# Perceiver of two layers: the loops of three attention phases written out, and layer 0's first norm moved from VectorE to ScalarE and GpSimd

## What is computed

```python
def _layernorm(x, axis=-1, eps=1e-05):
    m = jnp.mean(x, axis=axis, keepdims=True)
    v = jnp.var(x, axis=axis, keepdims=True)
    return (x - m) / jnp.sqrt(v + eps)

x = x + _L0_xattn_ref(_layernorm(x), ctx_1024, 32, ...)   # one head, softmax over the 32 largest of 257 scores
x = x + _L0_attn_ref(_layernorm(x), ...)                  # 16 heads of 8, rotary positions
x = x + _L0_ffn_ref(_layernorm(x), ...)                   # 8 experts, one each
x = x + _L1_xattn_ref(_layernorm(x), ctx_1024, ctx_1024, ...)
x = x + _L1_attn_ref(_layernorm(x), ...)                  # 16 heads of 64, behind a further RMS norm
x = x + _L1_ffn_ref(_layernorm(x), ...)                   # 8 experts, two each
```

## Time and profile before

| | before |
|---|---|
| median of 3 runs | 1502.33 us (1502.33 to 1504.12) |
| the profiled execution | 1503.75 us |
| its span, first to last instruction | 1502.0 us |
| busy in the span: TensorE, its weight loads | 1330.2 us (89%), 1020.1 us (68%) |
| VectorE, ScalarE, GpSimd | 1056.0 us (70%), 817.4 us (54%), 684.0 us (46%) |
| granted TensorE clock, mean | 0.957 of full speed |

### The profile page before, as it was taken

How to read it: one execution, slowest core, us unless ns; L and a number is a source line. 1 busy time by engine, 2 the same in 40 slices (tenths; PEclk the granted TensorE clock), 3 DMA queues, 4 the chain that set the end, 5 groups by cost and what they waited for, 6 DMA issues and landing times. The chain is left out here.

```text
span 1502.0 us, 42305 instructions
## 1 busy us (share of the span) xinstructions
PE 1330.2 (89%) x14710; PEld 1020.1 (68%) x14710; DVE 1056.0 (70%) x3440; ACT 817.4 (54%) x2416; POOL 684.0 (46%) x1301
## 2 busy tenths in 40 slices
PE   3888888877899969999999999978999999986981
PEld 2666666664577847777777777757788878875960
DVE  3889999864712258888888888865788888784433
ACT  2556665543223348888888888854444444443640
POOL 1455555531156724444444444541224444545773
PEclk9999999997999979999999999999999999997995
DMA  6655643301011132222222222200000000002425
GB/s 191 198 162 178 205 152 121 108 18 57 15 32 33 34 121 80 69 79 72 77 83 65 84 80 69 80 27 2 2 1 12 14 14 11 21 21 80 114 78 174
DMA packets 78431, 113.92 MB, mean 76 GB/s; under 512 B 12480, under 2 KB 55753, under 8 KB 78160
## 3 DMA queue, kind: packets, MB, share of 16 engines
q1 hardware_dynamic: 70352, 97.93, 20.2%
q0 software_dynamic: 6784, 12.06, 2.6%
q10 hardware_dynamic: 1152, 2.10, 0.4%
HBM read 78.95 MB, written 35.00 MB: 76 GB/s over the span
## 5 line engine op out<-in xcount | busy, mean ns | idle before, releaser
L1825 ACT ACTIVATE c_pr<-c_pS,c_nm 128x257 f32<-128x257 f32 x512 | 236.3, 475 | 74.8 <-DVE c_nm L1955 74.2
L1955 DVE TENSOR_REDUCE c_nm<-c_pS 128x1 f32<-128x257 f32 (+1 forms) x384 | 173.4, 507 | 29.9 <-PE c_pS L1694 29.9
L2303 ACT ACTIVATE s_k<-s_pK 128x512 f32<-128x512 f32 x128 | 76.4, 597 | 154.3 <-PE s_pK L2189 154.3
L2189 PEld LDWEIGHTS s_pK<-s_hT,AH 128*128 128x128 f32 x1024 | 123.9, 195 | 20.6 <-ACT s_k L2303 16.7
L2189 PE MATMUL s_pK<-s_hT,AH 128*128 128x128 f32 x1024 | 137.4, 284 | 0.5 <-ACT s_hT L2298 0.5
L1698 PE MATMUL c_pT<-cst,c_pr 128*128 128x128 f32 x1024 | 132.8, 273 | 0.0
L1698 PEld LDWEIGHTS c_pT<-cst,c_pr 128*128 128x128 f32 x1024 | 116.1, 141 | 0.4 <-issue 0.4
L1964 DVE COPY c_prT<-c_pT 128x512 f32<-128x512 f32 x128 | 88.5, 691 | 22.9 <-PE c_pT L1698 22.7
L1825 ACT ACTIVATION_READ_ACCUMULATOR c_pr<-c_pS,c_nm 128x1 f32 x512 | 104.0, 203 | 0.0
L2216 PE MATMUL s_pM<-BH,s_uT 128*128 128x128 f32 x832 | 98.2, 275 | 0.0
L2216 PEld LDWEIGHTS s_pM<-BH,s_uT 128*128 128x128 f32 x832 | 95.5, 192 | 0.0
(11 more groups left out here) (388 smaller groups left out, 3375.2 us busy)
## 6 DMA issues: line engine op xcount, KB each, us to landing
rows_in<-c_blank SPq DMA_DIRECT2D x32, 520.0 KB, 3.3
a_ctxT<-in_ctxT SPq DMA_DIRECT2D x32, 514.0 KB, 3.6
c_ctxT<-in_ctxT SPq DMA_DIRECT2D x128, 128.5 KB, 2.2
a_ctxN<-in_ctxR SPq DMA_DIRECT2D x32, 512.0 KB, 4.3
hb<-rows_in SPq DMA_DIRECT2D x39, 130.0 KB, 2.3
f_w<-in_f_w SPq DMA_DIRECT2D x16, 256.0 KB, 3.4
a_ctxL<-in_ctxL SPq DMA_DIRECT2D x128, 16.0 KB, 3.7
f_w<-in_f_w SPq DMA_DIRECT2D x16, 128.0 KB, 3.4
```

Source lines behind the costliest of these rows:

```text
L1825: act.activation(pr[:, b % 2, c, :], pS[:, c, 0:S], ACT.Exp, bias=nm[:, c:c + 1], accum_out=den[:, b % 2, c:c + 1]).then_inc(e_ready.sem, 1)
L1955: dve.tensor_reduce(nm[:, c:end], pS[:, c:end, 0:S], AX.X, ALU.max, negate=True).then_inc(max_ready.sem, 1)
L2189: mm = pe.matmul(pK[:, c % 2, i, :], AH[:, c * HK + i, :], hT[:, p, :], start=True, stop=True)
```

## The change

Three things change. In layer 0's attentions all 38 slots are written out, and SyncE's loop too; group numbers and semaphore values become constants. In layer 1's self-attention the five passes are written out. And the first norm of layer 0 is a `ScalarNorm`: ScalarE makes the negated mean and the sum of squared differences with the accumulator of an activation, GpSimd makes 1/sqrt(squares + 128 epsilon) and the shift, mean times that, and ScalarE scales. The missing factor sqrt(128) is put into the copy of the transposed result. VectorE loses three instructions a slot; it only prepares 128 epsilon once. ScalarE now waits at slot 1 for all of x too. On ScalarE the mean of w comes before the copy of the second norm (`normed_a`), the squares behind it, the scaling ahead of the exponentials. On GpSimd the norm step stays first in the slot.

```diff
+class ScalarNorm:
...
+        self.part, self.off = f("part", [P, D]), f("off", [P, D])
...
+    def scalar_mean(self, act, x):
+        act.activation(self.part[:, :], x, ACT.Copy, scale=-1.0 / D, accum_out=self.neg_mean[:, :]).then_inc(self.mean_ready.sem, 1)
+
+    def scalar_squares(self, act, x, r):
+        act.wait_ge(self.mean_ready.sem, self.mean_ready.at(r))
+        act.activation(self.off[:, :], x, ACT.Square, bias=self.neg_mean[:, :], accum_out=self.squares[:, :]).then_inc(self.squares_ready.sem, 1)
+
+    def vector_eps(self, dve):
+        dve.tensor_scalar(self.eps_d[:, :], self.env["k"]("eps"), float(D), None, ALU.mult).then_inc(self.eps_ready.sem, 1)
+
+    def gpsimd(self, pool, r):
+        if isinstance(r, int) and r == 0:
+            pool.wait_ge(self.eps_ready.sem, 1)
+        pool.wait_ge(self.squares_ready.sem, self.squares_ready.at(r))
+        pool.tensor_tensor(self.ve[:, :], self.squares[:, :], self.eps_d[:, :], ALU.add).then_inc(self.ve_ready.sem, 1)
+        pool.wait_ge(self.ve_ready.sem, self.ve_ready.at(r))
+        pool.tensor_tensor(self.rstd[:, :], self.ve[:, :], self.env["k"]("half"), ALU.pow).then_inc(self.rstd_ready.sem, 1)
+        pool.wait_ge(self.rstd_ready.sem, self.rstd_ready.at(r))
+        pool.tensor_tensor(self.shift[:, :], self.neg_mean[:, :], self.rstd[:, :], ALU.mult).then_inc(self.shift_ready.sem, 1)
+
+    def scalar_scale(self, act, x, r):
+        act.wait_ge(self.shift_ready.sem, self.shift_ready.at(r))
+        act.activation(self.h[:, :], x, ACT.Identity, bias=self.shift[:, :], scale=self.rstd[:, :]).then_inc(self.h_ready.sem, 1)
...
-        n1 = Norm(ctx, nc, "a_n1", env)
+        n1 = ScalarNorm(ctx, nc, "a_n1", env)
...
-            peeled = 6
-            for s in range(peeled):
-                slot(*groups(s), s % 2, s // 2)
-            pairs = (G - 1 - peeled) // 2
-            with eng.Fori(0, pairs) as i:
-                for s in (peeled, peeled + 1):
-                    slot(*(i * 2 + g for g in range(s + 1, s - 7, -1)), s % 2, i + s // 2)
-            for s in range(peeled + 2 * pairs, G + 6):
+            for s in range(G + 6):
                 slot(*groups(s), s % 2, s // 2)
...
-            with sp.Fori(1 + E, G // 2 - 1) as i:
+            for i in range(1 + E, G // 2 - 1):
...
-                act.activation(hT[:, :], pX[:, 0, :], ACT.Copy).then_inc(hT_ready.sem, 1)
+                act.activation(hT[:, :], pX[:, 0, :], ACT.Copy, scale=float(D) ** 0.5).then_inc(hT_ready.sem, 1)
...
+            def scale_w(w_):
+                if later(w_):
+                    act.wait_ge(hT_done.sem, hT_done.at(w_ - 1))
+                n1.scalar_scale(act, x_of(w_), w_)
...
             def slot(w_, x, t, u, a, b, z, l, p, r):
+                if isinstance(x, int) and x == 1:
+                    act.wait_ge(env["rest_loaded"], 4 * 16)
...
                 run(turned_weights, u)
+                run(lambda g: n1.scalar_mean(act, x_of(g)), w_)
                 run(lambda a: normed_a(a, p), a)
+                run(lambda g: n1.scalar_squares(act, x_of(g), g), w_)
                 run(sums, u)
...
                 run(queries_by_keys, x)
+                run(scale_w, w_)
                 run(exponentials, t)
...
+            n1.scalar_mean(act, X[:, 0, :])
+            n1.scalar_squares(act, X[:, 0, :], 0)
+            scale_w(0)
             slots(act, slot)
...
-                run(lambda g: n1.vector_rows(dve, x_of(g)), w_)
...
-                run(lambda g: n1.vector_moments(dve, g), w_)
...
-                run(scale_w, w_)
...
-            n1.vector_stats(dve, X[:, 0, :], 0)
-            scale_w(0)
+            n1.vector_eps(dve)
             slots(dve, slot)
...
-            with eng.Fori(1, 6) as i:
+            for i in range(1, 6):
                 for j in range(4):
                     slot(i * 4 + (5 + j), (5 + j) % 2, False, False, True, j, i)
```

More of the change, by code:

```diff
@@ L229, in vector_scale, with __init__ @@
                           ).then_inc(self.h_ready.sem, 1)
+class ScalarNorm:
+    def __init__(self, ctx, nc, name, env):
+        self.env = env
+        f = lambda n, s: ctx.enter_context(nc.sbuf_tensor(f"{name}_{n}", s, F32))
+        self.part, self.off = f("part", [P, D]), f("off", [P, D])
+        self.neg_mean, self.squares, self.ve, self.rstd, self.shift = (f(n, [P, 1]) for n in ("neg_mean", "squares", "ve", "rstd", "shift"))
+        self.eps_d, self.eps_ready = f("eps_d", [P, 1]), Signal(ctx, nc, f"{name}_eps_ready")
+        self.h = f("h", [P, D])
+        self.mean_ready, self.squares_ready = Signal(ctx, nc, f"{name}_mean_ready"), Signal(ctx, nc, f"{name}_squares_ready")
+        self.ve_ready, self.rstd_ready = Signal(ctx, nc, f"{name}_ve_ready"), Signal(ctx, nc, f"{name}_rstd_ready")
+        self.shift_ready, self.h_ready = Signal(ctx, nc, f"{name}_shift_ready"), Signal(ctx, nc, f"{name}_h_ready")
+    def scalar_mean(self, act, x):
[17 more added lines that the diff above has]
+        act.activation(self.h[:, :], x, ACT.Identity, bias=self.shift[:, :], scale=self.rstd[:, :]).then_inc(self.h_ready.sem, 1)
@@ L616, in keep_logits, with x_of @@
                 act.activation(LG[:, bass.ds(z, 1), :].rearrange("p g e -> p (g e)"), pB[:, 2, 0:E], ACT.Copy).then_inc(lg_ready.sem, 1)
+            def x_of(g):
+                return X[:, bass.ds(g, 1), :].rearrange("p g d -> p (g d)")
+            def scale_w(w_):
+                if later(w_):
+                    act.wait_ge(hT_done.sem, hT_done.at(w_ - 1))
+                n1.scalar_scale(act, x_of(w_), w_)
             def slot(w_, x, t, u, a, b, z, l, p, r):
+                if isinstance(x, int) and x == 1:
+                    act.wait_ge(env["rest_loaded"], 4 * 16)
                 run(turned_self_weights, z)
@@ L693, in x_of @@
                 return X[:, bass.ds(g, 1), :].rearrange("p g d -> p (g d)")
-            def scale_w(w_):
-                if later(w_):
-                    dve.wait_ge(hT_done.sem, hT_done.at(w_ - 1))
-                n1.vector_scale(dve, x_of(w_), w_)
             def largest(i):
```

## The result

The changed kernel takes 1491.1 us (median of 4 runs, 1487.79 to 1492.84) against 1503.22 for the kernel before on the same chip: ratio 0.9902, 95% interval 0.9875 to 0.9929. Two later series of six runs gave 0.9885 (0.986 to 0.9909) and 0.9892 (0.9872 to 0.9912). The forecast, 1484.4 of 1502.33, is 0.9881: inside all three intervals, on the faster side of their middle.

The account below looks back on a forecast made before the run. Layer 0's slot was bound by two legs, scale_z to rotation on TensorE and rotation to scale_z on VectorE. Gains 17.4 + 1.1 + 0.1 = 18.6 us gave 1485.1 or 1483.7; forecast 1484.4, between them, range 1480 to 1492.

Parts of the forecast that it names:

- (a): Layer 0's slots 7 to 31 without loop turns, slow slots and loop exit: 11.4 us gained.
- (b): First norm off VectorE in layer 0: its scaling leaves the rotation-to-scale_z leg, 0.25 us a slot, x 24 = 6.0.
- (c): ScalarE's added mean, squares and scaling, 1.48 us a slot, all hide in its idle gaps; nothing starts later.
- (d): GpSimd's longer norm chain still ends before the rotated sum, with 0.14 us to spare: the thinnest cover.
- (e): Start: group 0's norm waits for a table load and two ScalarE passes; counted 0, bounds -0.6 to +1.
- (f): Layer 1's self-attention written out: 0.1 us counted for the loop's entry, bounds -0.5 to +0.7.
- (g): Fetching the straight code: counted 0, upper end 0.56 us a slot.
- Rival 5: The fetch of straight code is not hidden: 13.4 us back, 1497.8; chance 0.03.
- (1): ScalarE's or GpSimd's share does not fit and the norm's gain is given back: 1491.7; chance 0.15.
- (2): The low clock stays, other waits bringing it as often; 3.1 us comes back: 1487.5; chance 0.1.
- (3): Squares need another activation table, two loads a slot on ScalarE: slower, 1518 to 1564; chance 0.03.
- (4): ScalarE's 1.48 us a slot lie on the path in full: 38 us lost, 1529; chance 0.01.

Follow-up runs that it names:

- unroll_only: The kernel before with its loops written out and the first norm left on VectorE; ratio 0.9962 to the kernel before.
- pe_loop_late: The changed kernel with the factor matrices loaded late and the loop back on TensorE alone; ratio 0.994 to the kernel before.
- pe_act_out: factors_late with the loops back on VectorE, GpSimd, SyncE and in layer 1; ratio 0.9918 to the kernel before.
- factors_late: The changed kernel with the loads of the two factor matrices moved to the end of SyncE's layer 0 list; ratio 0.9888 to the kernel before.
- norm_only: The changed kernel with loops back on TensorE, VectorE, GpSimd, SyncE and in layer 1, only ScalarE's list written out; ratio 0.9927 to the kernel before.
- again: The changed kernel run once more, unaltered; ratio 0.9885 to the kernel before.
- act_extra: The changed kernel with three more unused 128x128 copies on ScalarE in every slot; single run 1491.05 us.
- pool_extra: The changed kernel with one more unused 128x1 power on GpSimd in every slot, ahead of the norm's own; single run 1493.12 us.
- again_2: The changed kernel run a third time, unaltered; ratio 0.9892 to the kernel before.

## Why the prediction was right, and where its steps were off

The mechanism was right: two legs to a slot, the third norm's scaling between them, 8.70 without the first norm. Measured: 8.69, with legs of 3.64 and 5.05 where 3.66 and 5.04 were forecast. The whole came out higher than forecast by 2.7 us in the profiled execution (1487.79 for 1485.1), by the 2.9 given back behind layer 1's last slot. That the gain up to rotation 31 met its sum, 18.67 for 18.5, is luck: slots 7 to 31 gave 2.2 less than forecast, and what lies ahead of them 2.4 more.

- **(a)** "Layer 0 without a loop", 11.4: 10.65 in unroll_only. TensorE's loop by itself brings the turn back (pe_loop_late), and the loops of VectorE, GpSimd and SyncE bring none (pe_act_out); ScalarE's was not tried by itself. The 0.09 that a plain slot loses with the loops is on the VectorE leg. Mis-stated was the low clock: the slow slots also go with the norm alone, and one of the two was not there in a second profile of before. As it is in the gains of both parts, they can't simply be added: 10.65 + 8.97 - 3.08 = 16.5; factors_late, without the stall, measures 16.9.
- **(b)** 0.25 a slot: 0.245 in norm_only, 0.25 from unroll_only to the changed kernel. In the medians of one chip the shares came out the other way round, though: the loops alone brought 6.1 us (unroll_only), the norm 10.7 (norm_only), of 17.3 for both (again), where the sums of the prediction have 11.5 and 7.1. Part of it is the low clock: 3.1 us of it went with the norm alone, and unroll_only's profile has 6.5 more behind layer 0.
- **(c)** nothing on ScalarE: right. The scaling took 0.49, near its upper end. The mean with its read took 0.38 and the squares with theirs 0.48, both below their ranges, as a read starts before its activation ends. The gaps held three more copies of 0.30 each (act_extra).
- **(d)** "the thinnest cover": right, with 0.34 to spare, not 0.14, because the squares and their read end 0.38 behind the copy, not 0.60; past it the slot grows (pool_extra). One sign of being wrong was ill chosen: the bias add does start behind the rotation, by 0.11, but so it does in the sum of (d) itself (303.50 for 303.19). What counts is the rotated sum.
- **(e)** the start, counted as 0 with -0.6 to +1: rotation 3 came 1.00 earlier, and slots 3 to 6 gave 2.49 for 1.1. Of this 1.0 is low clock that I had not looked at: in the first profile of the kernel before the clock is 0.50 from 46.4 to 49.8 us, and in the changed kernel's first it is not. Against again_2 and factors_late, which have such a stretch near 47 us too, those slots gave 1.5. The gain ahead of rotation 3 was not explained.
- **(f)** layer 1, 0.1 gained: four slots lost 0.09 each, one gained 0.05 and one near the end 0.11, 0.2 lost.
- **(g)** is the step that failed: "Straight code has to be fetched", counted at 0. It cost 0.13 + 0.18 + 0.31 + 0.04 + 0.11 = 0.8 in five slots, which come with the written-out lists of VectorE and GpSimd, and 1.7 to 2.2 in slot 18, where TensorE's fetch stood behind 2 MB of factor matrices. The slots that I judged by, 31 and 32 of before, have no such load beside them. With these 2.5 the 17.4 of slots 7 to 31 become 14.9; measured 15.2. Rival 5 had the mechanism but not its form: not in each slot, but where a fetch falls due while large loads fill the queues, and not in each such place (unroll_only). Of this the Trainium skill (Runtime: NRT & Kernel Launch, Instruction fetch mechanics) says that the cost of crossing into the next 16 KiB block of code is mostly hidden: true of most of the 27 fetches of TensorE from 90 to 280 us, not of this one.
- **Rivals.** (1) did not come about: GpSimd and ScalarE have 0.34 us and more left. (2) not from 41 to 314 us, where the clock stays at 1.00; but lower clock behind layer 0 took 2.9 us in the first profile (behind layer 1's last slot) and 1.6 in that of factors_late (in the first slot of layer 1's self-attention). I had argued with the clock in the loop alone. (3) and (4) fell: one table load, and but for slot 18, where TensorE stops, no slot from 7 to 30 is longer than before.

## What to carry to other kernels

When a loop is written out, list the large transfers that run beside the new straight code: a fetch that falls due among them can stop an engine for 1 to 2 us, and moving the transfer moves or removes the stall. It need not stop: with the fetch 1.0 and 1.3 us behind the loads' issue there was no stall (unroll_only, factors_late). Cost a step that goes by the leg of the cycle on which it stands, in a slot of the same trace that already lacks it; that gave 8.70 for 8.69. And do not put down a slow stretch at lower clock to the code that is to go before a second profile shows it at the same place.

## What the runs showed that I had not expected

VectorE's scaling of 128x128 by two pointer scalars takes 0.34 us, but 0.98 when it starts 0.15 behind the start of GpSimd's 128x512 product; it ends 0.09 behind that product's end. VectorE's other work beside the same product in the changed kernel (maxima, replacements, statistics) kept its durations to 0.02. The Trainium skill (Advanced Engine Details and Errata, GPSIMD Details) says that GpSimd shares a read and a write interface with VectorE and conflicts with VectorE's instructions in a 2-port mode or with two SBUF inputs; the trace agrees that they conflict, 0.98 for 0.34, and no run shows which of the two cases this is.

Loops on VectorE and GpSimd cost 0.15 us in every slot although neither shows a turn of its own (pe_act_out); what in their lists takes the time was not tried. And profiles of the same program gain or lose 2 to 4 us at single places through longer or shorter stretches at granted clock 0.50: at the start of layer 1's cross-attention (the expectation of again_2 puts it at a feed-forward), at the start of its self-attention and behind its last slot. All profiles have such a stretch at these three changes of phase; what decides its length stays open.
